# The setup's weight preparation: tap sums on TensorE, half of the low halves on GpSimd, row products read in PSUM

## The reference

```
# layer 0: a C2f-like block with attention
t = silu(bn(conv1x1(x, cv1_w)));  ys = [t[:, :256], t[:, 256:]]
for i in range(2):
    z = silu(bn(conv3x3(ys[-1], m_cv1_w[i])))              # 256 -> 256
    z = attention(z, m_qkv_w[i], m_rw[i] + m_rh[i])        # 4 heads of 64, 1024 positions
    ys.append(ys[-1] + silu(bn(conv1x1(z, m_cv2_w[i]))))
y = silu(bn(conv1x1(concat(ys), cv2_w)))
# layer 1: a grouped 1x1 convolution, groups by argmax of S and T
s, t = argmax(softmax(S)), argmax(softmax(T))              # with their gains
w_eff = conv * t_gain[:, None] * (t[:, None] == s[None, :])
dense = conv1x1(x * s_gain, w_eff);  p = argsort(t);  return dense[:, p[p]]
```

## Time and profile before

| | us |
|---|---|
| median of 3 runs | 3112.66 (3112.54 to 3113.22) |
| the profiled execution | 3110.56 |
| its span | 3108.4 |
| first product of image 0 starts (in the span) | 149.91 |
| busy in the span: TensorE, VectorE, ScalarE, GpSimd | 2882.4, 1949.1, 1733.6, 1130.0 |
| waits of over 5 us in the setup: TensorE for the masked products, SyncE's load of group 8 to its landing | 17.6, 11.96 |

### The profile page before, as it was taken

How to read it: one execution, slowest core, us unless ns; L and a number is a source line. 1 busy time by engine, 2 the same in 40 slices (tenths; PEclk the granted TensorE clock), 3 DMA queues, 4 the chain that set the end, 5 groups by cost and what they waited for, 6 DMA issues and landing times.

```text
span 3108.4 us, 62540 instructions
## 1 busy us (share of the span) xinstructions
PE 2882.4 (93%) x27616; PEld 1580.7 (51%) x27616; DVE 1949.1 (63%) x2612; ACT 1733.6 (56%) x2176; POOL 1130.0 (36%) x790
## 2 busy tenths in 40 slices
PE   3699999999998999999999999999999999999997
PEld 2355454554555545654545545555456545465453
DVE  7676566756567465764657656674657656566564
ACT  3448383565646575383834747365654748438381
POOL 2235342443226261362523434153413616115151
PEclk7799999999999999999999999999999999999998
DMA  5110101101010010201002010100101001010001
GB/s 174 70 58 2 42 12 51 53 2 42 25 58 32 2 42 28 85 2 41 5 25 85 2 41 15 68 32 1 42 28 55 32 1 42 28 58 2 1 12 44
DMA packets 35902, 111.98 MB, mean 36 GB/s; under 512 B 12976, under 2 KB 15024, under 8 KB 32944
## 3 DMA queue, kind: packets, MB, share of 16 engines
q1 hardware_dynamic: 35632, 107.98, 9.7%
HBM read 85.69 MB, written 22.28 MB: 35 GB/s over the span
## 4 chain that ended last, share of the span: by engine, by line
PE 71%; ACT 11%; DVE 10%; issue 3%; POOL 3%; DMA 1%; SPq 0%; POOLq 0%; DVEq 0%
PE ps_u L856 39%; PE ps_u L1027 10%; PE ps_u L870 7%; DVE row_max L1471 4%; PE ps_o L1048 4%; PE ps_u L1001 3%; ACT wide L1224 3%; PE ps_o L1049 3%; ACT ps_u L1224 3%; PE ps_o L1050 3%; POOL y_rest L1604 1%; ACT probs L1228 1%; DVE wide L1245 1%; POOL z L1604 1%; ACT qk L1203 1%
## 5 line engine op out<-in xcount | busy, mean ns | idle before, releaser
L1471 DVE TENSOR_REDUCE row_max<-ps_u 128x2 f32<-128x1024 f32 x512 | 618.0, 1221 | 225.9 <-PE ps_u L1001 225.9
L1626 POOL TENSOR_TENSOR probs<-wide,probs 128x1024 f16<-128x1024 f32 x256 | 544.9, 2129 | 171.0 <-ACT probs L1228 160.4
L1093 ACT ACTIVATE wide<-ps_u,par_t 128x512 f32<-128x512 f32 x224 | 173.6, 775 | 537.8 <-PE ps_u L856 498.0
L1027 PE MATMUL ps_u<-qk 64*128 64x512 f16 x3072 | 418.7, 378 | 44.1 <-ACT wide L1224 20.3
L1048 PEld LDWEIGHTS ps_o<-v_ext,probs 128*128 128x128 f16 x4096 | 374.9, 96 | 161.5 <-issue 129.0
L1048 PE MATMUL ps_o<-v_ext,probs 128*128 128x65 f16 x4096 | 431.7, 193 | 0.9
L1049 PE MATMUL ps_o<-v_ext,probs 128*128 128x64 f16 x4096 | 429.1, 195 | 0.0
L1050 PE MATMUL ps_o<-v_ext,probs 128*128 128x65 f16 x4096 | 426.5, 191 | 0.0
L856 PE MATMUL ps_u<-y_pad,w_c 128*128 128x512 f16 x1728 | 394.1, 383 | 0.0
L1049 PEld LDWEIGHTS ps_o<-v_ext,probs 128*128 128x128 f16 x4096 | 380.5, 97 | 6.2
L1245 DVE SCALAR_TENSOR_TENSOR wide<-wide 128x512 f32<-128x512 f32 x256 | 176.6, 692 | 328.2 <-ACT wide L1094 310.4
(11 more groups left out here) (209 smaller groups left out, 4394.6 us busy)
## 6 DMA issues: line engine op xcount, KB each, us to landing
w_c<-w_c_dram SPq DMA_DIRECT2D x7, 3072.0 KB, 9.9
w_c<-w_c_dram SPq DMA_DIRECT2D x8, 2304.0 KB, 8.8
xn<-in_x_dram SPq DMA_DIRECT2D x32, 512.0 KB, 6.0
o_nat<-in_x_dram SPq DMA_DIRECT2D x64, 256.0 KB, 2.7
out_dram<-qk SPq DMA_DIRECT2D x32, 512.0 KB, 2.6
probs<-in_L_conv_m_cv_w_dram SPq DMA_DIRECT2D x3, 1152.0 KB, 8.7
w_c_dram<-w_c SPq DMA_DIRECT2D x1, 3072.0 KB, 9.8
w_c_dram<-w_c SPq DMA_DIRECT2D x1, 2304.0 KB, 7.9
```

The costliest lines, as they stand in the source:

```text
L1027: ins = e.matmul(ps_u[:, use.slot + q, :], lhsT, rhs, start=k == 0, stop=k == 3)
L1471: e.reduce_max(row_max[:, g % 2, :, it, half], ps_u[:, use.slot:use.slot + 2, :], axis=AX.X).then_inc(*dve_max.up(i, b, g, half, it))
L1626: e.tensor_tensor(p_part(s, 1), wide[:, w.slot, :], p_part(s, 0), ALU.subtract).then_inc(*pool_lo.up("p", i, b, s))
```

## The change

- `l1_keys` stands ahead of the scale of group 1.
- Groups 4 and 5: no sums on GpSimd. TensorE makes the planes of a dy by f32 products with an identity, `ident`, and its negative, `minus_ident` (new, made once by GpSimd): one product each for the two end planes, three each, accumulated in PSUM, for the two sums. They need the group's scaling alone.
- From group 3 on, banks with odd k (`on_pool`, 13 in all) get their low half from GpSimd: ScalarE copies the bank to `wide` in f32 as well, and GpSimd subtracts. Those PSUM banks are free when ScalarE has copied them.
- `l1_masks` directly behind `l1_ranks`; `l1_rows` one group earlier (behind groups 3 to 6), in the two rows of `ps_o` by turns, read there by VectorE's maximum and by ScalarE's high half, without `wf`. The low half is a step of its own, `l1_lo`, one group later, and reads PSUM too.
- `bn_products` split from `bn_tables`, one group later.
- `l1_unit` from the end to behind group 7; `l1_weights` wait for it.

```
@@ -267,7 +267,7 @@
 s_row, g_row = tmp(C), tmp(C)
-row_l1 = tmp(4)
+row_l1 = tmp(2, 4)
@@ -278,7 +278,7 @@
 row_diag = yp[:, 4 * C:6 * C].bitcast(F32).rearrange("p (t k) -> p t k", t=CT)
-tap_sums = w_cv2[:, :, :, :].rearrange("p a b c -> p (a b c)")[:, 0:8 * 3 * CH].bitcast(F32).rearrange("p (g j c d) -> p g j c d", g=2, j=2, d=3)
+minus_ident = w_cv2[:, :, :, :].rearrange("p a b c -> p (a b c)")[:, 0:2 * P].bitcast(F32)
@@ -333,12 +333,19 @@
+def on_pool(g, k):
...
+    return g >= 3 and k % 2 == 1
...
     for k, bank in enumerate(banks_of(GROUPS[g])):
-        plan("w_bank", g, k, bank, setup_ring.take(("act_cast", ("w", g, k)), ("dve_lo", ("w", g, k))))
+        use, w = setup_ring.take(("act_cast", ("w", g, k)), *([] if on_pool(g, k) else [("dve_lo", ("w", g, k))])), None
+        if on_pool(g, k):
+            w = wide_ring.take(("pool_lo", ("w", g, k)))
+        plan("w_bank", g, k, bank, use, w)
@@ -351,19 +358,17 @@
     plan("w_apply", 0)
+    plan("l1_keys")
     plan_group_scale(1)
-    plan("l1_keys")
...
         plan_group_banks(g)
-        if g + 1 < len(GROUPS) and not by_plane(g + 1):
+        if g + 1 < len(GROUPS):
...
             plan_group_scale(g + 2)
-            if by_plane(g + 2):
-                plan("w_apply", g + 2)
@@ -377,17 +382,21 @@
             plan("l1_ranks")
-        if g == 3:
...
         if 4 <= g < 4 + CT:
-            plan("l1_rows", g - 4)
+            plan("l1_lo", g - 4)
+        if 3 <= g < 3 + CT:
+            plan("l1_rows", g - 3)
...
             plan("bn_tables")
+        if g == 6:
+            plan("bn_products")
+        if g == 7:
+            plan("l1_unit")
...
     plan("r_operands")
-    plan("l1_unit")
@@ -803,19 +812,25 @@
+def as_bank(g, bank, flat):
...
+    m0, ms, q0, qs = bank
+    src = flat[:, 0:ms * qs * P]
+    return src.rearrange("p (m k o) -> p m k o", m=2, k=2) if ms == 2 else src.rearrange("p (q o) -> p q o", o=P)
...
     m0, ms, q0, qs = bank
-    src = setup_bank(use.slot)[:, 0:ms * qs * P]
+    src = as_bank(g, bank, setup_bank(use.slot))
     if name == "c3":
-        return taps_of(at[0])[:, part, q0:q0 + qs, at[1] * P:(at[1] + 1) * P], src.rearrange("p (q o) -> p q o", o=P)
+        return taps_of(at[0])[:, part, q0:q0 + qs, at[1] * P:(at[1] + 1) * P], src
...
         dst = w_qkv[:, at[0], part, :, m0 * P:(m0 + 2) * P] if name == "qkv" else w_m2[:, m0 // HT, part, :, :]
-        return dst.rearrange("p k (m o) -> p m k o", m=2), src.rearrange("p (m k o) -> p m k o", m=2, k=2)
+        return dst.rearrange("p k (m o) -> p m k o", m=2), src
...
     m = at[0] + m0
-    return dst[:, part, q0:q0 + qs, m * P:(m + 1) * P], src.rearrange("p (q o) -> p q o", o=P)
+    return dst[:, part, q0:q0 + qs, m * P:(m + 1) * P], src
@@ -872,24 +887,26 @@
         if kind == "w_bank":
-            g, k, (m0, ms, q0, qs), use = a
+            g, k, (m0, ms, q0, qs), use, w = a
...
             once(got_stage[g % 3], g)
-            if by_plane(g):
-                once(pool_small, "tap_sums", g)
-            else:
-                once(act_cast, "scaled", g)
+            once(act_cast, "scaled", g)
...
                 for q in range(q0, q0 + qs):
+                    o = setup_bank(use.slot)[:, n * P:(n + 1) * P]
                     if by_plane(g):
-                        cols, (dy, unit_at) = slice(q // UNITS * P, (q // UNITS + 1) * P), divmod(q % UNITS, PLANES)
-                        w = src[:, m, cols, 3 * dy + 2 * unit_at] if unit_at < 2 else tap_sums[:, g % 2, unit_at - 2, cols, dy]
+                        cols, (dy, plane_at) = slice(q // UNITS * P, (q // UNITS + 1) * P), divmod(q % UNITS, PLANES)
+                        w0, w1, w2 = (src[:, m, cols, 3 * dy + dx] for dx in range(3))
+                        once(pool_small, "minus_ident")
+                        if plane_at < 2:
+                            ins = products(o, [((w0, minus_ident), (w2, ident[:, :]))[plane_at]])
+                        else:
+                            ins = products(o, [(w0, ident[:, :]), (w2, ident[:, :]), (w1, (ident[:, :], minus_ident)[plane_at - 2])])
                     else:
-                        w = src[:, m, q // taps * P:(q // taps + 1) * P, q % taps]
-                    ins = e.transpose(setup_bank(use.slot)[:, n * P:(n + 1) * P], w, ident[:, :])
+                        ins = e.transpose(o, src[:, m, q // taps * P:(q // taps + 1) * P, q % taps], ident[:, :])
@@ -904,15 +921,16 @@
             once(dve_small, "gn_var", 0, 0)
-            if m:
-                e.wait_ge(*dve_small.at("l1_wf", m - 1))
+            if m > 1:
+                e.wait_ge(*dve_small.at("l1_split", m - 2))
             for t in range(CT):
-                ins = e.matmul(ps_o[:, 0, :], one_hot[:, t, m * P:(m + 1) * P], wl[:, t, :], start=t == 0, stop=t == CT - 1)
+                ins = e.matmul(ps_o[:, m % 2, :], one_hot[:, t, m * P:(m + 1) * P], wl[:, t, :], start=t == 0, stop=t == CT - 1)
...
             once(dve_small, "l1_split", CT - 1)
+            once(dve_small, "l1_unit")
@@ -920,7 +938,8 @@
         elif kind == "l1_unit":
-            e.wait_ge(*act_cast.at("w_l1", CT - 1, 0))
+            once(dve_small, "l1_split", CT - 2)
+            once(dve_small, "l1_split", CT - 1)
@@ -933,9 +952,10 @@
         elif kind == "setup_end":
-            for k in range(len(banks_of(GROUPS[-1]))):
-                once(act_cast, "w", len(GROUPS) - 1, k)
-                once(dve_lo, "w", len(GROUPS) - 1, k)
+            g = len(GROUPS) - 1
+            for k in range(len(banks_of(GROUPS[g]))):
+                once(act_cast, "w", g, k)
+                once(*((pool_lo,) if on_pool(g, k) else (dve_lo,)), "w", g, k)
@@ -1106,11 +1126,14 @@
         if kind == "w_bank":
-            g, k, bank, use = a
+            g, k, bank, use, w = a
...
             dst, src = w_bank(g, bank, use, 0)
+            if w:
+                until_free(e, w)
+                e.activation(as_bank(g, bank, wide[:, w.slot, :]), src, ACT.Copy)
@@ -1121,11 +1144,8 @@
             m, = a
-            f = row_l1[:, 3:4]
             e.wait_ge(*dve_small.at("l1_factor", m))
-            e.activation(wf, wf, ACT.Copy, scale=f).then_inc(*act_cast.up("l1_scaled", m))
-            e.wait_ge(*act_cast.now())
-            e.activation(v_split[:, m, 0, :], wf, ACT.Copy).then_inc(*act_cast.up("l1_hi", m))
+            e.activation(v_split[:, m, 0, :], ps_o[:, m % 2, :], ACT.Copy, scale=row_l1[:, m % 2, 3:4]).then_inc(*act_cast.up("l1_hi", m))
@@ -1282,7 +1302,9 @@
         elif kind == "w_bank":
-            g, k, bank, use = a
+            g, k, bank, use, w = a
+            if w:
+                continue
@@ -1320,21 +1342,21 @@
             e.wait_ge(*o_full.at("l1_rows", m))
-            if m:
-                e.wait_ge(*act_cast.at("l1_hi", m - 1))
-            e.tensor_copy(wf, ps_o[:, 0, :]).then_inc(*dve_small.up("l1_wf", m))
-            e.wait_ge(*dve_small.now())
-            r = row_l1.unsqueeze(2)
-            small(e.tensor_reduce(r[:, 0, :], wf, AX.X, ALU.max, apply_absolute_value=True))
+            r = row_l1[:, m % 2, :].unsqueeze(2)
+            small(e.tensor_reduce(r[:, 0, :], ps_o[:, m % 2, :], AX.X, ALU.max, apply_absolute_value=True))
...
             e.tensor_scalar(r[:, 3, :], r[:, 2, :], WEIGHT_TOP, None, ALU.mult).then_inc(*dve_small.up("l1_factor", m))
+        elif kind == "l1_lo":
+            m, = a
             e.wait_ge(*act_cast.at("l1_hi", m))
-            e.tensor_tensor(v_split[:, m, 1, :], wf, v_split[:, m, 0, :], ALU.subtract).then_inc(*dve_small.up("l1_split", m))
-            e.wait_ge(*dve_small.now())
+            e.scalar_tensor_tensor(v_split[:, m, 1, :], ps_o[:, m % 2, :], row_l1[:, m % 2, 3:4], v_split[:, m, 0, :],
+                                   ALU.mult, ALU.subtract).then_inc(*dve_small.up("l1_split", m))
...
             e.tensor_scalar(t[:, 0, :], raw[:, 3, :], BN_EPS, None, ALU.add).then_inc(*dve_small.up("bn_var"))
+        elif kind == "bn_products":
+            t, raw = bn_tmp, bn_raw
@@ -1349,7 +1371,7 @@
             e.wait_ge(*o_full.at("l1_unit"))
-            e.tensor_scalar(l1_unit[:, :], ps_o[:, 0, 0:CT], 1.0 / WS, None, ALU.mult)
+            e.tensor_scalar(l1_unit[:, :], ps_o[:, 0, 0:CT], 1.0 / WS, None, ALU.mult).then_inc(*dve_small.up("l1_unit"))
@@ -1539,6 +1561,7 @@
             e.memset(minus_half[:, :], -0.5)
+            e.tensor_scalar(minus_ident, ident[:, :], -1.0, 0.0, ALU.mult, ALU.add).then_inc(*pool_small.up("minus_ident"))
@@ -1550,16 +1573,14 @@
             small(e.iota(iota_k, pattern=[[1, C]], base=0, channel_multiplier=0, allow_small_or_imprecise_dtypes=True), "iota")
+        elif kind == "w_bank":
+            g, k, bank, use, w = a
+            if w:
+                e.wait_ge(*act_cast.at("w", g, k))
+                e.tensor_tensor(w_bank(g, bank, use, 1)[0], as_bank(g, bank, wide[:, w.slot, :]), w_bank(g, bank, use, 0)[0],
+                                ALU.subtract).then_inc(*pool_lo.up("w", g, k))
...
```

(16 more changed lines are left out.)

## The result

The changed kernel took 3134.41 us (median of 4 runs, 3133.77 to 3135.85), the kernel before 3112.60 beside it: a ratio of 1.0073, 95% interval 1.0060 to 1.0086. It is slower by 22 us. The forecast was 3114, with a range of 3106 to 3121.

What follows compares the result with a forecast made beforehand. TensorE, busy 93% of the span, was taken as the bound, with time following image 0's first product one for one; -0.3 us (landing) and +1.6 (tail) gave +1.3, so 3114 us for the median, range 3106 to 3121.

Steps and rivals of the forecast that it cites:

- Parts 1 and 2: Setup on VectorE: keys before group 1's scale, -4.0 us; ranks without GpSimd's tap sums beside them, another -4.6 us.
- Part 3: Masks directly behind ranks: last masked product ends at 72.1 us (lower bound 68.8), so first row products start 20 us earlier.
- Part 4: Tap sums of groups 4 and 5 on TensorE: 11.0 us a group for 2.8, TensorE setting the end there.
- Part 5: Low halves on GpSimd: write-back at 105.8 us, 0.3 earlier; group 8's load lands at 118.2, VectorE stands 6.7.
- Part 6: Tail from group 8's landing to image 0's first product: 151.2 us against 149.9, +1.3; unit products 5.7.
- The sum: Whole kernel: -0.3 us at the landing and +1.6 in the tail make +1.3, 3114 us for the median.
- half clock in groups 4 and 5: Rival: TensorE at half clock through both groups, 19 us on top, 3133 us; chance 5%.
- The sums are nearly free: Rival: TensorE's sum products run as transposes do, 5.5 us a group, tail 10 us earlier, 3104 us; chance 6%.
- as forecast: Case that the walk through the new queues holds for the whole kernel, 3114 us; chance 65%.

Runs made afterwards that it cites:

- e1: Changed kernel with groups 4 and 5's products taking 128 neighbouring stage columns, not every ninth (wrong taps): 3110.79 us, ratio 0.9999 to the kernel before.
- e2: Changed kernel with stationary columns at steps 2, 3, 4 (group 4) and 6, 8, 16 (group 5), wrong taps: 3127.96 us in one execution.
- e3: Changed kernel with SyncE issuing group 8's load ahead of the write-back of bottleneck 0's taps: 3127.06 us, ratio 1.0052 to the kernel before.
- e4: Changed kernel with GpSimd's tap sums and TensorE's plain transposes put back: 3106.80 us, ratio 0.9985 to the kernel before.
- e10: e7 with all low halves on VectorE, none on GpSimd: 3095.86 us, ratio 0.9953 to the kernel before.
- e7: e4 with group 8's load ahead of the write-back and the unit products behind group 8's transposes: 3099.02 us, ratio 0.9963 to the kernel before.
- e11: Changed kernel with all low halves on VectorE, none on GpSimd: 3132.19 us, ratio 1.0069 to the kernel before.
- e9: Kernel before the change with only the tap sums moved from GpSimd to TensorE: 3119.15 us, ratio 1.0023 to the kernel before.
- e5: Changed kernel with ScalarE's scaling of groups 4 and 5 writing tap by tap, so stationary columns are neighbours: 3113.43 us, ratio 1.0008 to the kernel before.
- e8: e5 with group 8's load ahead of the write-back and the unit products behind group 8's banks: 3104.57 us, ratio 0.9975 to the kernel before.
- e12: e10 with the unit products back at the end of the setup: 3094.98 us, ratio 0.9944 to the kernel before.

## Why the prediction was wrong

By its own steps, forecast against the changed kernel's trace:

- **Parts 1 and 2, right.** The scale of group 2 at 22.8 (23.0), the ranks 55.4 to 61.9 (55.7 to 62.2).
- **Part 3, right.** The last masked product ends at 71.5 (72.1). L1339 stretches to 1.59 beside GpSimd, as taken.
- **Part 4, wrong in one term.** "A group costs 96 x 0.115 = 11.0 us" measured 22.8 and 23.1 us. The count of 96 was right, the granted clock of 1.0 too. The duration was put together from two rows that each had half of it: L892 has the step of nine but is a transpose, L900 is an f32 product but with neighbouring columns. No row had an f32 product with a step, and the bound from above, 0.133, came from the second row alone. e1 and e2 show the missing factor: the step from one to four elements doubles the pitch. The two groups are 24.0 us over the forecast, and that is nearly the whole miss up to the write-back (24.2). The first row products took 6.62, not 5.6 (5.14 to 6.78 in the runs), from a start 0.5 earlier than forecast.
- **Part 5, right.** From the end of TensorE's products to the write-back 2.4 us (2.45), landing 12.1 us after the issue, VectorE's stand 6.7 (6.7); e3 took it away and gained 6.5.
- **Part 6, near.** From the landing to the first product 34.4 us (33.0): the unit products took 6.96 from idle, not 5.7, with the clock at 0.50 throughout (153.4 to 160.3).
- **The sum.** The first product is 25.7 us later than forecast (24.3 at the landing, 1.4 in the tail). The opening sentence, that the time moves with that start one for one, was not quite right: the span behind it was 1.3 shorter than before, since image 0 begins at full clock. The median is 20.4 over. The other 4 us have no cause in the prediction: 0.4 less around the span, and the profiled execution lay 1.4 above its median, where that of before lay 2.1 below.

The rival "half clock in groups 4 and 5" gave 3133, close to the time, by luck: the trace excludes its mechanism, since the clock was at full. It had the right 192 instructions, at 0.215 us each (0.115 and 0.1 more), where 0.239 was measured. "The sums are nearly free" was out on the count. The case for "as forecast" was e1, and that kernel does run in the time of the one before (0.9999).

The Trainium skill, "Perfetto Trace Analysis", section "Transposes", advises transposes for logical transposes and not ordinary matmuls. The runs agree, more sharply than the prediction priced it: the same 128x128 strided block is one instruction of 0.115 as a transpose and two of 0.239 as a product. The lock that the Trainium skill states in "SBUF — State Buffer", section "Who interferes with whom", decided part 3 rightly: VectorE's mask from 65.50 took 1.59 us for 0.54 beside GpSimd's product of 65.54 to 66.80, and the last product ended at 71.5, near 72.1 and not 68.8.

Of the change, then: the sums on TensorE lose 28 us against GpSimd's (e4), 24 of them by the step (e1). Without them the rest gains some 4 us (e4): the write-back is 4.4 us earlier than in the kernel before, and image 0 begins at full clock. Within that rest GpSimd's low halves lose 3 to 5 us (e10 against e7), and 2 in the trace of the change as it stands (e11). What the earlier keys, masks and row products gain one by one is read from the traces only, and whether the unit products are better ahead of group 8 or at the end the times don't tell.

## What to carry to other kernels

The price of an instruction is that of its operation and its access pattern together; when the trace has one row for the operation and another for the pattern, the product of the two is unknown, and the bound from above must allow the slower pattern to double the slower operation. Behind a long wait for a load, look at what stands ahead of it in its queue before speeding up what comes before: moving one step in SyncE's queue was worth 6 us here, more than the 4 that the change gained outside the sums. Strided f32 reads are best taken out where they are cheap or hidden; here transposes kept their pitch with a step and products did not. And a piece of work moved out of the setup can change the clock with which the next stage begins: look at the first instructions behind the part that you changed, too.

## What the runs showed of the hardware

- An f32 product's stationary columns at a step of 1, 2, 3, 4, 6, 8, 9, 16 elements: 0.112, 0.119, 0.174, 0.233, 0.223, 0.238, 0.239, 0.218 us an instruction of 128 columns, at full clock (e1, e2, the changed kernel). At step nine it is 0.239 at half clock as at full (e9). A transpose with step nine: 0.115 at full clock (before).
- ScalarE reading f32 at a step of nine elements: 4.44 us for 2304 a partition (e5), 2.2 side by side.
- The granted clock stayed at 0.50 through 14 us in which TensorE's records (transposes, products of one column, then products of layer 1) nearly fill the time (e7), and through the 12 from 154 to 166 in the changed kernel. In e8's profiled execution, with the same order of work, it rose to 1.00 by 126.5 us, while the unit products ran, and was 0.50 behind them (129.7 to 132.0). So the same order of work doesn't always meet the same clock.
- With the clock at full, it fell to 0.50 during 32 f32 products of one column, with TensorE's records busy throughout (e12, 129.3 to 134.3), and the first 96 products of image 0 behind them took 22.8 us for 20.9.
